# Stacked q and k: a feature's three copies in adjacent partitions instead of blocks of 16

## What is computed

```python
xn = layernorm(x)
q = rms_norm(heads(xn @ Wq.T), qn_w)      # 16 heads of 16 features
k = rms_norm(heads(xn @ Wk.T), kn_w)
v = heads(xn @ Wv.T)
attn = softmax(q @ k.T * 16 ** -0.5)
a = merge(attn @ v) @ Wo.T
# the tokens are sorted by a balanced routing over 8 experts, each takes its
# 1024 best of those left, then: routed + gelu(layernorm(routed) @ w1 + b1) @ w2 + b2
out = x + a + experts(xn)
```

## Time and profile before

| | |
|---|---|
| timed runs | 1098.56, 1101.88, 1103.78 us; median 1101.88 |
| profiled execution | 1093.31 us, span 1091.6 us |
| granted TensorE clock | 0.994 of full speed |
| TensorE busy | 1039.5 us, 95% of the span |
| VectorE, ScalarE, GpSimd | 77%, 68%, 65% |
| DMA | 138.17 MB, 127 GB/s on average |
| reads of line 324 | 372 of 128 KB and 24 of 64 KB |

### The profile page before, as it was taken

The page is one execution under the profiler, slowest core; times in us unless marked ns, Lnnn a source line. Parts: engine busy times, 40 slices in busy tenths (PEclk is TensorE's granted clock), DMA queues, the critical chain, the costliest instruction groups (busy, mean ns, idle before and its releaser), DMA issues.

```text
span 1091.6 us, 20994 instructions
## 1 busy us (share of the span) xinstructions
PE 1039.5 (95%) x7222; PEld 671.5 (62%) x7222; DVE 843.8 (77%) x1893; ACT 745.5 (68%) x966; POOL 714.5 (65%) x753
## 2 busy tenths in 40 slices
PE   4899999999999999999999997999999999999997
PEld 3445555444444444444444442489988899998897
DVE  8899886777887788787887678697768776776861
ACT  3688888788788878887778786875546555455550
POOL 5677888677666757676756755657676576766334
PEclk9899999999999999999999999999999999999999
DMA  4777977776766876767767868234435243443313
GB/s 154 182 161 143 229 156 147 164 141 122 169 131 127 171 139 117 177 118 133 168 128 132 175 137 210 86 102 88 99 81 129 50 112 82 95 124 58 64 20 39
DMA packets 86698, 138.17 MB, mean 127 GB/s; under 512 B 13104, under 2 KB 38960, under 8 KB 86576
## 3 DMA queue, kind: packets, MB, share of 16 engines
q1 hardware_dynamic: 57728, 103.06, 43.6%
q0 software_dynamic: 12288, 16.79, 9.2%
q10 hardware_dynamic: 16560, 16.78, 6.1%
HBM read 86.25 MB, written 50.33 MB: 125 GB/s over the span
## 4 chain that ended last, share of the span: by engine, by line
PE 72%; DVE 11%; issue 5%; DMA 3%; ACT 3%; POOL 2%; SPq 2%; ACTq 0%; POOLq 0%; DVEq 0%
PE W L1475 17%; PE S L1461 16%; PE pv L505 13%; PE S L490 10%; PE W L449 8%; DMA stq<-parts 3%; PE W L460 3%; ACT prob L705 2%; PE W L474 2%; SPq L324 2%; DVE ge L932 1%; PE R L419 1%; DVE best L942 1%; DVE raw L837 1%; PE R L1447 1%
## 5 line engine op out<-in xcount | busy, mean ns | idle before, releaser
L705 ACT ACTIVATE prob<-S 128x1024 f32<-128x1024 f32 x512 | 498.3, 1022 | 120.7 <-PE S L490 119.6
L505 PE MATMUL pv<-prob,v 128*17 128x512 f32 x2048 | 248.4, 599 | 1.5 <-DVE oT L870 1.2
L490 PE MATMUL S<-stq,stk 64*128 64x512 f32 x1024 | 201.3, 457 | 16.0 <-ACT prob L705 6.7
L490 PEld LDWEIGHTS S<-stq,stk 64*128 64x128 f32 x1024 | 84.2, 185 | 146.3 <-ACT prob L705 110.0
L1737 POOL DMA_INDIRECT out<-prob,order_rows x64 | 106.0, 1656 | 48.0 <-DVE prob L1677 37.1
L1200 POOL TENSOR_TENSOR sq<-raw 128x512 f32<-128x512 f32 x62 | 64.5, 1042 | 88.3 <-DVE raw L837 55.1
L505 PEld LDWEIGHTS pv<-prob,v 128*17 128x17 f32 x2048 | 46.3, 96 | 118.8 <-issue 116.7
L1537 ACT ACTIVATE wq_act<-S,b 128x512 f32<-128x512 f32 x64 | 43.9, 685 | 93.9 <-PE S L1461 93.6
L1461 PE MATMUL S<-raw_nT,xT_w 128*128 128x512 f32 x384 | 91.1, 395 | 0.0
L1230 POOL TENSOR_TENSOR lo<-full,hi 128x512 fp32r<-128x512 f32 x62 | 80.0, 1290 | 5.0
L1461 PEld LDWEIGHTS S<-raw_nT,xT_w 128*128 128x128 f32 x384 | 71.6, 188 | 17.7 <-issue 1.7
(11 more groups left out here) (257 smaller groups left out, 2595.9 us busy)
## 6 DMA issues: line engine op xcount, KB each, us to landing
stk<-parts SPq DMA_DIRECT2D x186, 128.0 KB, 4.5
stq<-parts SPq DMA_DIRECT2D x186, 128.0 KB, 7.0
xT<-in_w SPq DMA_DIRECT2D x32, 512.0 KB, 4.8
parts<-hi SPq DMA_DIRECT2D x63, 256.0 KB, 2.2
parts<-lo SPq DMA_DIRECT2D x63, 256.0 KB, 2.1
out<-ao ACTq DMA_DIRECT2D x32, 256.0 KB, 5.1
xb<-in_x ACTq DMA_DIRECT2D x13, 512.0 KB, 5.5
xb<-in_x SPq DMA_DIRECT2D x2, 512.0 KB, 5.0
```

The source lines that it names most:

```text
L490: ins = e.matmul(S[n % 2][:, h, :], stack["k"][u][64 * h:64 * h + 64, p, c * P:(c + 1) * P], stack["q"][u][64 * h:64 * h + 64, p, :], star ...
L505: ins = e.matmul(pv[32 * j:32 * j + VW, :], v[b % 2][:, c, 8 * u + 4 * g + j, :], prob[(2 * t + j // 2) % RING][:, j % 2, :], start=(c == ...
L705: e.activation(prob[n % RING][:, :, :], S[n % 2][:, :, :], ACT.Exp).then_inc(s_exp, 1)
```

## The change

Row r of a feature's four is now next to the others: feature i of the 32 in a pair (head h = i // 16) has its copies in partitions 4i, 4i + 1 and 4i + 2, and the spare row in 4i + 3. A copy therefore goes to partitions r, r + 4, ..., r + 124, for both heads with one transfer of 32 partitions x 4 pairs x 2 KB = 256 KB, and a half takes six transfers. The semaphores count 96 instead of 192. Spare rows are no longer a block, so the shifts go into row 4i + 3 of the first two features; `shift_sync` first zeroes them from the last use, and `shift_tensor` multiplies over all 64 rows instead of 48. All that is in the branch.

```diff
@@ put_part
         if nb and part == "hi" and n == "k":
-            e.wait_ge(s_stack[u], 192 * nb)
+            e.wait_ge(s_stack[u], 96 * nb)
@@ stack_rows
     def stack_rows(e, u, n, part, r, pairs=slice(0, 4), done=None):
-        src = parts_dram[u, "qk".index(n), part].rearrange("(p e d) n -> e d p n", e=2, d=DH)
-        for h in range(2):
-            e.dma_start(stack[n][u][64 * h + DH * r:64 * h + DH * (r + 1), pairs, :].bitcast(F32),
-                        src[h][:, pairs, :]).then_inc(done or s_stack[u], 16)
+
+        src = parts_dram[u, "qk".index(n), part].rearrange("(p e) n -> e p n", e=2 * DH)
+        e.dma_start(stack[n][u][r:P:4, pairs, :].bitcast(F32), src[:, pairs, :]).then_inc(done or s_stack[u], 16)
@@ shift_sync
+        at = [(i, h, 64 * h + 4 * i + 3) for i in range(2) for h in range(2)]
+        src = [shift_dram[i].rearrange("(p e c) q -> e p (c q)", e=2, c=CH) for i in range(2)]
+        e.dma_start(shift_dram.rearrange("i r (a b) -> (i r a) b", b=NT), zero[:, :]).then_inc(g_zero, 16)
+        e.wait_ge(g_zero, 80 * n + 16)
+        for i, h, row in at:
+            e.dma_start(stack["q"][u][row:row + 1, :, :].bitcast(F32), src[i][h:h + 1]).then_inc(g_zero, 16)
+        e.wait_ge(g_zero, 80 * (n + 1))
         e.wait_ge(g_shl, n + 1)
...
-        for i in range(2):
-            src = shift_dram[i].rearrange("(p e c) q -> e p (c q)", e=2, c=CH)
-            for h in range(2):
-                row = 64 * h + 48 + i
-                e.dma_start(stack["q"][u][row:row + 1, :, :].bitcast(F32), src[h:h + 1]).then_inc(g_in, 16)
+        for i, h, row in at:
+            e.dma_start(stack["q"][u][row:row + 1, :, :].bitcast(F32), src[i][h:h + 1]).then_inc(g_in, 16)
@@ heads (and the same in tensor_program, in the branch)
         if n == 0:
-            e.wait_ge(c_stack, 192)
+            e.wait_ge(c_stack, 96)
         elif hs % 16 == 0 or n == 8:
-            e.wait_ge(s_stack[u], 192 * (b + 1))
+            e.wait_ge(s_stack[u], 96 * (b + 1))
@@ shift_tensor
+        e.wait_ge(g_zero, 80 * (n + 1))
...
-                ins = e.matmul(S[i % 2][:, h, :], stack["q"][u][64 * h:64 * h + 48, p, c * P:(c + 1) * P],
-                               stack["k"][u][64 * h:64 * h + 48, p, :], start=True, stop=True)
+                ins = e.matmul(S[i % 2][:, h, :], stack["q"][u][64 * h:64 * h + 64, p, c * P:(c + 1) * P],
+                               stack["k"][u][64 * h:64 * h + 64, p, :], start=True, stop=True)
```

More of the change, by code:

```diff
@@ L268, in attention_and_routing @@
     s_out = [sem(f"s_out{i}") for i in range(2)]
-    g_mm, g_red, g_neg, g_turn, g_shf, g_shh, g_shl, g_out, g_in = (
-        sem(f"g_{n}") for n in ("mm", "red", "neg", "turn", "shf", "shh", "shl", "out", "in"))
+    g_mm, g_red, g_neg, g_turn, g_shf, g_shh, g_shl, g_out, g_in, g_zero = (
+        sem(f"g_{n}") for n in ("mm", "red", "neg", "turn", "shf", "shh", "shl", "out", "in", "zero"))
     r_split, r_key, r_ge, r_pc, r_cnt, r_dg, r_best, r_ch, r_tie, r_sel, r_rank, r_place, r_last, r_iota, r_eq, r_hot, r_order, r_kept = (
```

## The result

| | before | changed |
|---|---|---|
| median of 4 timed runs | 1101.7 us (1098.56 to 1103.78) | 1089.38 us (1087.84 to 1090.92) |
| ratio, 95% interval | | 0.9891 [0.9861, 0.992] |
| the same pair in a second session | 1095.86 us | 1092.6 us; 0.9958 [0.9932, 0.9984] |
| the same pair in a third session | 1092.22 us | 1084.03 us; 0.9927 [0.9905, 0.995] |

The forecast of 1095.2 us was 5.8 us too high; the measured time lies in its range. But the first two intervals don't meet. The mean of the three ratios is 0.9925, some 8 us.

A forecast was written before the change was run, and what follows sets the result against it. TensorE, busy 95% of the span, was taken as the bound; only its 6.0 to 7.1 us of waits for copies could go. Taking 6.6 off the profiled 1093.31, in proportion from 1101.88, gave 1095.2 us, range 1087 to 1102.

The forecast's parts named there:

- Step 1: SP's issuing: six reads of 256 KB for twelve save 2.7 us per load, by itself worth nothing.
- Step 2: Stack loads: every-fourth-partition destinations drain in 4 to 6 us, so the load from 198.78 us lands at 203 to 206.
- B: Rival: the copies' landing doesn't move, since DRAM reading or packets set the rate; 1101.9 us, chance 0.14.
- Step 3: TensorE's four stalls for the copies: loads 8 to 10 us shorter end them whole, worth 6.6 us.
- Nothing else is late next: After the stalls: VectorE, itself waiting for TensorE 2.6 us in all, has no backlog to eat the gain.
- Rival C: VectorE's routing chain is reached earlier and 3 us go into longer TensorE stalls there; 1098.2 us, chance 0.12.
- A+: Rival: timed runs have longer loads and more, deeper copy stalls, also removed; 1087 to 1093 us, chance 0.17.
- A: Main case: the stall for the copies goes and nothing else; 1095.2 us, own range 1093 to 1097, chance 0.48.
- D: Rival: strided writes meet at the same SBUF places and drain slower than 12.3 us; 1120 us, chance 0.09.
- Steps 4 to 6: The kernel's start, the semaphore waits, the unused branch with the shifts, and the heads' score matmuls: each worth nothing.
- What would show it: Trace signs: reads landing in 2.5 to 5 us, loads of 5 to 8, lower DMA share, no copy waits.
- The warning for step 3: Sign of error: the DMA wait is gone but TensorE's waits for VectorE or ScalarE have grown several us.

The follow-up runs named there:

- spread_only: The changed kernel's every-fourth-partition destinations, but still one 128 KB read per head, twelve a load: 1083.99 us, 0.9914 of the kernel before.
- late3: The changed kernel with three 2 KB transfers, each waited for, holding back q's reads in each load: 1111.36 us, 1.0138 of the kernel before.
- no_reads: Stacks loaded once, in the first batch, then kept with no further reads or waits; writes to DRAM stay: 1083.28 us, 0.9917 of the kernel before.
- same_again: The kernel before, run again unaltered: 1092.67 us against 1093.1, ratio 0.9988.
- after_third: The changed kernel, run unaltered for the third time, in the third session: 1084.03 us, 0.9927 of the kernel before.
- after_again: The changed kernel, run again unaltered in the second session: 1092.60 us, 0.9958 of the kernel before.

## Why the prediction came out as it did

- **Step 1, six reads for twelve: worth nothing by itself.** Right: spread_only has twelve and is as fast. Its size was wrong: I saved six issues of 0.45 us, 2.7; the strided ones take 0.63, so 5.5 us became 3.8.
- **Step 2, the drain.** The mechanism was right: destination, not bytes, packets or DRAM, set the rate. What it is in a destination that sets it, no run shows. B falls. The size was a little off: I took 4 to 6 us of drain and a landing at 203 to 206 us, measured 207.6, with 5.6 us of drain (5.1 on average); I had counted it from 198.78, and 3.2 us of issuing stand before it. My loads of 5 to 8 us measured 8.5.
- **Step 3, the stall goes whole, 6.6 us.** Shown by the trace (no wait on the copies in any run with the new form but late3), by no_reads (nothing more to gain) and by late3 (it comes back). "If barely" was right as well: same_again had six stalls, not four, one of 0.71 us at 169.3, where the first trace had 0.1 us to spare.
- **Nothing else is late next; VectorE has no backlog.** This is the step that failed in size, and with it the 5.8 us. I read the two waits for counts as fixed costs of the routing that would move neither way. They hold 3.8 to 8.9 us of TensorE's time with the old form of the update, by how VectorE's two-tensor operations fall on GpSimd's, and 2.4 to 3.7 with the new one. The first profile of the changed kernel had 2.1 us less of them than before, after_third 3.7, after_again 1.4 more. Rival C's mechanism, that coming earlier changes VectorE's chain, was there, but mostly the other way: less waiting, where C had 3 us more.
- **The sum.** 6.6 us in proportion is a ratio of 0.9940. It lies inside the intervals of the second and third session and above that of the first. The forecast is nearest to the third, 0.9927. In its profile, 10.2 us of span are 1.3 at the start and 8.8 in the stage, where 6.0 of copies and 3.7 of counts went and 0.9 came back otherwise, and 0.1 after it. How much of the first session's 12.3 us is the same scatter isn't known: its timed runs left no trace of the kernel before.
- **A+** came nearest to the time, for a reason that is not its own: no run shows longer loads. A's own range, 1093 to 1097, missed the 1089.38; that the whole range held it was luck as far as the mechanism goes. In executions as long as the 1098 to 1104 us of the result A+ stays untested.
- **D** falls: the strided form is faster than any other.
- **Steps 4 to 6** (start, waits, branch, heads) cost nothing, as said. The start came 1.3 us earlier in two of the three executions, with TensorE's granted clock and not with the copies: from 42 to 46 us it was 0.72 of full speed (2.4 GHz) on average in the kernel before and 1.00 in after_third, but 1.00 in same_again as well.
- **What would show it.** Reads at 3.5 and 4.4 us (2.5 to 5 foretold), no DMA in waits and chain, a DMA share lower by two to four tenths: all seen. The warning for step 3, a wait for VectorE grown by several us, did not come true; the largest growth is 1.4 us, in after_again.

The rule weighed as B's support ("DMA: Bandwidth & Descriptors", Rules for kernel authors, of the Trainium skill) says that transfers to disjoint halves serialize. Read as a price for the change it misled: in spread_only, whose twelve reads alternate between the halves as they did before, 237 GB/s were moved against 128, because each is spread within its half. Its advice, one 128-partition transfer, was not tried as such; reads to 32 partitions spread over all 128 moved 308.

## What to carry to other kernels

Where a transfer is slow with its DMA engines fully busy, compare the GB/s of two stretches at the same share, and look at which partitions the destination takes; spreading it may do what merging is meant to do. Before pricing a stall by its wait alone, ask how far its transfer is from being in time: a change elsewhere can end a stall of 1 to 2 us, and two repairs of the same edge don't add up. And where a small VectorE operation on the chain shows a maximum eight times its minimum, look at what GpSimd does beside it, and give it one tensor and scalars.

## What the runs showed of the hardware

- Read rate by destination, same bytes and source, in one load each: 128 GB/s (blocks of 16 partitions), 216 (32 in a row), 237 or more (every fourth of 64, held back by issuing), 308 (every fourth of 128). Mean length of a load in this order: 13.5, 9.8, 10.3, 8.5 us.
- Issuing a read with a strided destination takes SP 0.6 us for 128 and for 256 KB; one to a block 0.43 to 0.46 for either.
- A 128x1 VectorE operation with two SBUF tensors: 0.16 us beside an idle GpSimd (19 of 19), up to 1.30 beside a busy one; with one tensor and two scalars 0.27, whatever GpSimd does (77 of 77).
- The same form of read moved 131 and 153 GB/s in the loads for the same half of two kernels, and ScalarE stood 2.7 to 4.3 us at the change of stages in five executions. Neither is explained.
